# Attention over the heads: four slabs of head sums added by an accumulating DMA, and denominators taken three units behind

## The reference, cut to what matters

```python
def _L0_attn_b_ref(x, Wq, bq, Wk, bk, Wv, bv, Wo, bo):
    B, S, E = x.shape
    H = N_HEADS                      # 16 heads of D = 8
    D = E // H
    q = (x @ Wq.T + bq).reshape(B, S, H, D)
    k = (x @ Wk.T + bk).reshape(B, S, H, D)
    v = (x @ Wv.T + bv).reshape(B, S, H, D)
    scores = jnp.einsum('bqnd,bknd->bnqk', q, k) / jnp.sqrt(jnp.float32(D))
    attn = jax.nn.softmax(scores, axis=1)
    out = jnp.einsum('bnqk,bknd->bnqd', attn, v)
    out = out.transpose(0, 2, 1, 3).reshape(B, S, E)
    return out @ Wo.T + bo
```

## Time and profile before

| | us |
|---|---|
| median of 3 runs | 2010.51 |
| the profiled execution, its own time | 2014.26 |
| its span in the trace | 2012.4 |
| first and last L840 of the stage start at | 553.3 and 1691.9 |

### The profile page before, as it was taken

One profiled execution on the slowest core, in us unless ns is written; L12 is line 12 of the kernel. 1 busy time (PEld: TensorE's weight loads), 2 busy tenths in 40 slices (PEclk: granted clock), 3 DMA queues, 4 the chain that ended last, 5 costly groups with the idle time before them and its releaser, 6 DMA issues. The chain is left out here.

```text
span 2012.4 us, 54448 instructions
## 1 busy us (share of the span) xinstructions
PE 1915.1 (95%) x21688; PEld 1273.7 (63%) x21688; DVE 1715.0 (85%) x2601; ACT 1241.3 (62%) x2217; POOL 1547.4 (77%) x1180
## 2 busy tenths in 40 slices
PE   5998899999699999999999999999999998999998
PEld 3666644444367777777777777777777776544443
DVE  6776688886689999999999999999999997788876
ACT  4566456666466666666666666666666665566665
POOL 5255365656199999999999999999999997556565
PEclk8999799999799999999999999999999999799999
DMA  6744278564400000000000000000000000587762
GB/s 162 196 101 96 48 140 152 132 127 86 140 13 14 10 17 10 14 14 11 17 10 14 14 12 16 10 14 14 8 8 6 10 6 2 100 156 152 126 139 52
DMA packets 119886, 118.97 MB, mean 59 GB/s; under 512 B 50641, under 2 KB 82273, under 8 KB 118897
## 3 DMA queue, kind: packets, MB, share of 16 engines
q1 hardware_dynamic: 114112, 112.89, 25.9%
q10 hardware_dynamic: 5520, 2.60, 0.5%
HBM read 96.95 MB, written 18.55 MB: 57 GB/s over the span
## 5 line engine op out<-in xcount | busy, mean ns | idle before, releaser
L1099 DVE TENSOR_REDUCE head_shift<-head_score 128x64 bf16<-128x1024 f32 x512 | 624.1, 1219 | 81.8 <-PE head_score L883 69.8
L1056 ACT ACTIVATE head_ex<-head_score 128x1024 f32<-128x1024 f32 x512 | 524.7, 1025 | 185.3 <-PE head_score L905 183.5
L840 POOL TENSOR_TENSOR head_half<-head_ex 128x1024 f32<-128x1024 f32 x256 | 604.8, 2363 | 40.6 <-ACT head_ex L1056 40.6
L1355 POOL TENSOR_TENSOR ffn_sw<-ffn_sg,ffn_wide 128x512 f32<-128x512 f32 x256 | 325.0, 1269 | 218.7 <-ACT ffn_sg L1466 203.3
L1106 DVE TENSOR_TENSOR head_ex<-head_ex,head_recp 128x1536 f32<-128x1536 f32 x256 | 446.7, 1745 | 5.2 <-ACT head_recp L1028 5.2
L915 PE MATMUL head_den<-head_half,c_ident 128*128 128x128 f32 x3072 | 387.3, 276 | 2.5 <-POOL head_half L841 2.5
L915 PEld LDWEIGHTS head_den<-head_half,c_ident 128*128 128x128 f32 x3072 | 365.1, 193 | 6.0 <-POOL head_half L841 2.6
L847 POOL TENSOR_TENSOR head_ex<-head_ex,head_recip 128x512 f32<-128x512 f32 x256 | 329.0, 1285 | 22.6 <-ACT head_recip L1030 14.6
L905 PE MATMUL head_score<-head_shift,c_identb 128*128 128x512 bf16 x1024 | 310.0, 384 | 18.0 <-DVE head_shift L1099 12.0
L883 PE MATMUL head_score<-att_b_HB,att_b_GR 96*128 96x256 f16 x2048 | 311.5, 274 | 0.5 <-ACT head_ex L1056 0.5
L898 PE MATMUL head_outp<-head_ex,att_b_vs 128*32 128x128 f32 x8192 | 277.1, 276 | 0.0
(11 more groups left out here) (264 smaller groups left out, 2468.3 us busy)
## 6 DMA issues: line engine op xcount, KB each, us to landing
ffn_wide<-pair_weights SPq DMA_DIRECT2D x256, 256.0 KB, 9.7
band_v_windows<-a_values SPq DMA_DIRECT2D x24, 192.0 KB, 4.6
att_b_vs<-in_zero_f SPq DMA_DIRECT2D x2, 2176.0 KB, 10.2
a_keys<-band_parts_k SPq DMA_DIRECT2D x12, 295.5 KB, 2.5
att_a_HB<-a_keys SPq DMA_DIRECT2D x48, 73.9 KB
a_queries<-band_parts_q SPq DMA_DIRECT2D x12, 271.5 KB, 3.0
att_a_GR<-a_queries SPq DMA_DIRECT2D x12, 271.5 KB
b_queries<-head_parts_q SPq DMA_DIRECT2D x32, 96.0 KB, 1.6
```

Source lines behind the costliest of these rows:

```text
L840: ch.link(pool.tensor_tensor(hf, e[:, 0:8, :], e[:, 8:16, :], ALU.add))
L1056: act.activation(ex[:, kt % RING, :, h * QS:(h + 1) * QS], score[:, h, :, :].rearrange("p k (a w) -> p (k a) w", a=NH // 2), ACT.Exp, scal ...
L1099: dve.tensor_reduce(shift[:, h, :], score[:, h, :, :].rearrange("p k (a w) -> p w k a", a=NH // 2), AX.XY, ALU.max, negate=True).then_inc( ...
L1355: pool.tensor_tensor(sw[:, unit % 2, :], sg[:, unit % 2, :], wide[:, k % 2, i, :], ALU.mult).then_inc(sw_ready, 1)
```

## The change

The second sum on POOL (L841) goes. In its place POOL issues a DMA that adds slabs 4 to 7 of `half` onto its slabs 0 to 3, in SBUF, 512 f32 elements in each of 128 partitions (256 KB); the DMA engines do the addition. POOL issues it once its own first sum has been written (`half_ready`) and once the DMA of the unit before has landed (`quarters_added`). PE then waits for the DMA's semaphore and sums four slabs in place of six. LAG becomes 3, the ring of `ex` 5 buffers, and `half` 3 buffers (SUMS). The heads are stored in another order, so that the 12 slabs that DVE weighs and the 4 that POOL weighs each lie together; the numbers of elements stay as they were. PE's `attend` waits for POOL's four slabs before its 13th head, not before its 9th.

```diff
-    LAG, RING = 2, 4
-    ON_DVE = 3
-    SLABS = (0, 1, 4, 5, 6, 7)
+    LAG, RING, SUMS = 3, 5, 3
+    ON_DVE = 12
+    SLABS = range(NH // 4)
...
-            def sum_heads(unit, kt):
-
-                e, hf = ex[:, kt % RING, :, :], half[:, kt % 2, :, :]
-                ch = Chain(pool, pool_chain, unit)
+            def sum_heads(unit):
+
+                e, hf = ex[:, unit % RING, :, :], half[:, unit % SUMS, :, :]
                 pool.wait_ge(ex_ready, ONE + 2 * unit + 2)
-                pool.wait_ge(den_ready, ONE + unit)
-                ch.link(pool.tensor_tensor(hf, e[:, 0:8, :], e[:, 8:16, :], ALU.add))
-                pool.tensor_tensor(hf[:, 0:2, :], hf[:, 0:2, :], hf[:, 2:4, :], ALU.add).then_inc(quarter_ready, 1)
+                if unit >= SUMS:
+                    pool.wait_ge(den_ready, ONE + 1 + unit - SUMS + 1)
+                pool.tensor_tensor(hf, e[:, 0:8, :], e[:, 8:16, :], ALU.add).then_inc(half_ready, 1)
+                pool.wait_ge(half_ready, ONE + unit + 1)
+                if unit > 0:
+                    pool.wait_ge(quarters_added, unit * 16)
+                pool.dma_start(hf[:, 0:4, :], hf[:, 4:8, :], accum_op=ALU.add).then_inc(quarters_added, 16)
...
-                e = ex[:, kt % RING, :, :].rearrange("p (g a) q -> p g a q", a=GH)[:, :, ON_DVE, :]
-                pool.tensor_tensor(e, e, recip[:, kt % 2, :][:, None, :].broadcast_to([P, NG, P]),
+                e = ex[:, unit % RING, ON_DVE:NH, :]
+                pool.tensor_tensor(e, e, recip[:, unit % 2, :][:, None, :].broadcast_to([P, NH - ON_DVE, P]),
                                    ALU.mult).then_inc(rest_ready, 1)
...
-                    if i == HH:
+                    if i == ON_DVE:
                         pe.wait_ge(rest_ready, ONE + unit + 2)
...
-                pe.wait_ge(quarter_ready, ONE + unit + 1)
+                pe.wait_ge(quarters_added, (unit + 1) * 16)
                 pe.wait_ge(ln_done, ONE + unit)
                 for i, k in enumerate(SLABS):
-                    last = pe.matmul(den[:, 0:P], c["ident"][:, :], half[:, kt % 2, k, :], start=(i == 0), stop=(i == len(SLABS) - 1))
+                    last = pe.matmul(den[:, 0:P], c["ident"][:, :], half[:, unit % SUMS, k, :], start=(i == 0), stop=(i == len(SLABS) - 1))
```

More of the change, by code:

```diff
@@ L739, in head_softmax_attention @@
         ex = m.sb("ex", [P, RING, NH, P])
-        half = m.sb("half", [P, 2, NH // 2, P])
+        half = m.sb("half", [P, SUMS, NH // 2, P])
         recip = m.sb("recip", [P, 2, P])
@@ L832, in _, with weigh_rest @@
             m.start(pool, "pool")
[L834 to L837 removed]
+            def sum_heads(unit):
+                e, hf = ex[:, unit % RING, :, :], half[:, unit % SUMS, :, :]
                 pool.wait_ge(ex_ready, ONE + 2 * unit + 2)
[L839 to L843 removed]
+                if unit >= SUMS:
[5 more added lines that the diff above has]
+                pool.dma_start(hf[:, 0:4, :], hf[:, 4:8, :], accum_op=ALU.add).then_inc(quarters_added, 16)
+            def weigh_rest(unit):
                 pool.wait_ge(copy_ready, ONE + unit + 1)
[L846 to L847 removed]
+                e = ex[:, unit % RING, ON_DVE:NH, :]
+                pool.tensor_tensor(e, e, recip[:, unit % 2, :][:, None, :].broadcast_to([P, NH - ON_DVE, P]),
                                    ALU.mult).then_inc(rest_ready, 1)
@@ L853, in chunk_of @@
                     if not (first and kt < LAG):
-                        weigh_rest(unit - LAG, (kt - LAG) % BT)
-                    sum_heads(unit, kt)
+                        weigh_rest(unit - LAG)
+                    sum_heads(unit)
             chunk_of(0, True)
@@ L860, in _ @@
             for kt in range(BT - LAG, BT):
-                weigh_rest(LAST * BT + kt, kt)
+                weigh_rest(LAST * BT + kt)
         @block.tensor
@@ L897, in attend @@
                     at = n * VSLOT + VSLOT - D - n4 * D
-                    last = pe.matmul(outp[g * 32:(g + 1) * 32, 0:P], vs[:, buf * BT + kt, at:at + 32], ex[:, kt % RING, n, :],
+                    last = pe.matmul(outp[g * 32:(g + 1) * 32, 0:P], vs[:, buf * BT + kt, at:at + 32], ex[:, unit % RING, i, :],
                                      start=(kt == 0 and n4 == 0), stop=(kt == BT - 1 and n4 == GH - 1), skip_group_check=True)
@@ L908, in take_maximum, with denominator_of @@
                 last.then_inc(shifted, 1)
-            def denominator_of(unit, kt):
-                pe.wait_ge(quarter_ready, ONE + unit + 1)
+            def denominator_of(unit):
+                pe.wait_ge(quarters_added, (unit + 1) * 16)
                 pe.wait_ge(ln_done, ONE + unit)
                 for i, k in enumerate(SLABS):
-                    last = pe.matmul(den[:, 0:P], c["ident"][:, :], half[:, kt % 2, k, :], start=(i == 0), stop=(i == len(SLABS) - 1))
+                    last = pe.matmul(den[:, 0:P], c["ident"][:, :], half[:, unit % SUMS, k, :], start=(i == 0), stop=(i == len(SLABS) - 1))
                 last.then_inc(den_ready, 1)
@@ L952, in chunk_of @@
                     if not (first and kt < LAG):
-                        denominator_of(unit - LAG, (kt - LAG) % BT)
+                        denominator_of(unit - LAG)
                     if kt < BT - 1:
@@ L1019, in high_part, with reciprocal_of @@
                 return act.activation(parts, bank[:, None, :].broadcast_to([P, 2, cols]), ACT.Identity, bias=c["b_bias"][:, u:u + 1])
-            def reciprocal_of(unit, kt):
+            def reciprocal_of(unit):
                 act.wait_ge(copy_ready, ONE + unit)
@@ L1029, in reciprocal_of @@
                 act.wait_ge(rest_ready, ONE + unit)
-                act.activation(recip[:, kt % 2, :], lnd[:, :], ACT.Exp, scale=-1.0).then_inc(copy_ready, 1)
+                act.activation(recip[:, unit % 2, :], lnd[:, :], ACT.Exp, scale=-1.0).then_inc(copy_ready, 1)
             def copy_out(n):
@@ L1055, in chunk_of @@
                             act.wait_ge(av_done, ONE + unit)
-                        act.activation(ex[:, kt % RING, :, h * QS:(h + 1) * QS],
-                                       score[:, h, :, :].rearrange("p k (a w) -> p (k a) w", a=NH // 2),
+                        act.activation(ex[:, unit % RING, :, h * QS:(h + 1) * QS].rearrange("p (a g) w -> p g a w", g=NG),
+                                       score[:, h, :, :].rearrange("p k (g a w) -> p (k g) a w", a=GH, w=QS),
                                        ACT.Exp, scale=SCALE / ASCALE ** 2).then_inc(ex_ready, 1)
@@ L1061, in chunk_of @@
                         if h == 0 and not (first and kt < LAG):
-                            reciprocal_of(unit - LAG, (kt - LAG) % BT)
+                            reciprocal_of(unit - LAG)
                     ahead(b, q, kt)
@@ L1076, in _ @@
             for kt in range(BT - LAG, BT):
-                reciprocal_of(LAST * BT + kt, kt)
+                reciprocal_of(LAST * BT + kt)
             copy_out(LAST)
@@ L1100, in largest, with weigh @@
                                   AX.XY, ALU.max, negate=True).then_inc(shift_ready, 1)
-            def weigh(unit, kt):
+            def weigh(unit):
                 dve.wait_ge(recip_ready, ONE + unit + 2)
-                e = ex[:, kt % RING, :, :].rearrange("p (g a) q -> p g a q", a=GH)[:, :, 0:ON_DVE, :]
-                dve.tensor_tensor(e, e, recp[:, 0:P][:, None, None, :].broadcast_to([P, NG, ON_DVE, P]), ALU.mult).then_inc(prob_ready, 1)
+                e = ex[:, unit % RING, 0:ON_DVE, :]
+                dve.tensor_tensor(e, e, recp[:, 0:P][:, None, :].broadcast_to([P, ON_DVE, P]), ALU.mult).then_inc(prob_ready, 1)
             def add_output(n):
@@ L1150, in chunk_of @@
                     if not (first and kt < LAG):
-                        weigh(unit - LAG, (kt - LAG) % BT)
+                        weigh(unit - LAG)
                     ahead(b, q, kt)
@@ L1203, in _ @@
             for kt in range(BT - LAG, BT):
-                weigh(LAST * BT + kt, kt)
+                weigh(LAST * BT + kt)
             stats_of(LAST - 1)
```

6 lines of the change are left out of this document (3 added, 3 removed).

## The result

The changed kernel takes 2122.48 us (median of 4 runs, 2120.81 to 2123.71) against 2011.03 us before (median of 4 as well): a ratio of 1.055 (95% interval 1.054 to 1.057). The forecast was 2070 us, its own range 2025 to 2160 and the 8-in-10 range 1957 to 2230. The sign and the engine that sets the pace came out as forecast. The loss did not: 111 us, where the sum had 58.

A forecast was written before the change was run, and what follows sets the result against it. POOL alone was to bound the stage, at 4.68 us a unit against 4.465: 55 us over 255 distances plus 3 for edges, 2014.26 + 58 = 2072, less 3.75, say 2070 us; own range 2025 to 2160, 8-in-10 range 1957 to 2230.

The forecast's parts named there:

- PE's two matmuls: PE's denominator in each unit: four of six matmuls remain, 0.50 us less, so PE needs 3.91 us, not 4.41.
- PE's wait for the landing: PE's wait for the DMA before the denominator: some two units (9 us) remain for the landing, easier than POOL's wait.
- DVE's floor of 4.15 to 4.23: DVE's need per unit, 4.23 us with full projections and 4.15 in the last batch, the floor whatever POOL does.
- rival 1: Issue on POOL cheap or made beside its next instruction, DVE bounds: 1957 to 1960 us; chance 0.29 with its weaker form.
- I, the issue on POOL: Time one DMA issue holds POOL: 1.00 us taken, ends 0.34 and 3.5, making POOL's unit 3.68 + 1.00 = 4.68 us.
- the DMA needs the same wait: On POOL, the 0.08 us after L840 in which its write is awaited was taken to hold for the DMA too.
- the entries counted for the issue: POOL's issue: two reads and a write for each of 128 partitions, 384 entries at 2.13 ns, 0.18 + 0.82 us.
- The wait for the DMA before: POOL's wait before each issue: landing taken as 4.2 us against 4.68 between issues, 0.5 us of cover, so no cost.
- Edges: End of the stage: the last DMA costs 3.5 us more, two matmuls less give back 0.5; sum 3 us.
- 2: Rival: the landing takes over 4.68 us and sets the unit's length; at 5.3 us, 2228 us; chance 0.17.
- 3: Rival: the two prices on POOL cancel, issue between about 0.76 and 0.80 us; 2007 to 2014 us; chance 0.07.
- The signs: L840's distance near 4.68 us in all batches, gap to L847 1.0 us or more, DVE and PE about 90% and 83% busy.

The follow-up runs named there:

- no_dma: The changed kernel without the DMA and its wait, PE still summing four slabs, so half of the heads are missing from the denominator: 1970.49 us, ratio 0.9788.
- plain copy: The changed kernel with the same DMA without accumulation, so four slabs of sums are lost from the denominator: 2036.34 us in a single run.
- half_rows: The changed kernel with its DMA over 64 of the 128 partitions, the other half of the additions left out: 2100.63 us in a single run.
- two_flight: The changed kernel with each DMA waiting for that of two units before, not one, by two alternating semaphores: 2107.33 us, ratio to before 1.0474.
- dma_later: The changed kernel with POOL issuing each unit's DMA after its next product, the same instructions otherwise: 2039.42 us, ratio 1.0134.

## Why the prediction was right, and where its size was off

- **What bounds the stage.** Right: POOL alone after the change, PE and DVE with room. No_dma shows the cover: without the issue the same program ran at 4.30 us a unit.
- **PE's two matmuls.** Right in size, worth nothing: in the earlier trace rows the denominator was 1.50 us a unit, now 285.5 / 256 = 1.12 in the page, and PE waits 97.4 us for POOL. The 1.12 is spread by waits inside; an undisturbed one takes 1.06 us.
- **PE's wait for the landing.** The two units of cover weren't there: PE stood 42.2 us in 46 places for the DMA, in the rows above for the one that POOL had issued last. As POOL sets the pace, the other engines run ahead of it until they wait. It cost nothing, since POOL's product waited only 3.6 us for ACT.
- **DVE's floor of 4.15 to 4.23.** Never reached; 4.30 in no_dma. The allowance of 8 us for rival 1 was too small by about 10: it said 1957 to 1960, and no_dma took 1970.
- **I, the issue on POOL: the mis-sized term.** Put at 1.00 us; the undisturbed unit is 4.80 - 3.68 = 1.12. From the issue to the next start it is only 0.61 us. But from the start of L840 to the issue it is 2.95 us where it was 2.44 to L841: 0.29 for the late part of the issue before, which L840's end carries, and 0.22 for the longer wait (0.30 against 0.08). 0.61 + 0.29 + 0.22 = 1.12. The plain copy has the first and the last alone: 4.50 - 3.68 = 0.82, and 0.61 + 0.22 = 0.83. The step "the DMA needs the same wait" failed, and the entries counted for the issue weren't what it costs (half_rows), so 1.00 lay near by luck. 0.12 x 255 = 31 us of the miss.
- **The wait for the DMA before.** Put at nothing, with 0.5 us of cover below a landing of 4.2. It left out the 0.53 us at least that lie between a landing and the next issue's start: 4.2 + 0.53 = 4.73 would have been above its own 4.68. The median landing of 3.3 us saved it, which was luck. The tail reached 6.0 us, beside the 16 KB packets of the instruction queue. (4.882 - 4.80) x 255 = 21 us is what it and the waits without a name cost: beyond the usual 0.30 us, 20.5 - 20 x 0.30 = 14.5 in the 20 waits for a landing, which two_flight got back, and 7.6 - 6 x 0.30 = 5.8 in the six others, which it kept. One landing was compared with the room, where the longest should have been, with the time from landing to issue added.
- **Edges.** 2122.52 - 2014.26 = 108.3 us between the profiled executions, less (4.882 - 4.465) x 255 = 106.3, leaves 2; the sum had 3.
- **Added up.** 55 forecast + 31 + 21 = 107 of pace, against 106.3 measured.
- **Rivals.** 2 happened in part (15 us), 1 and 3 did not.
- **The signs.** The distance of L840 is 4.89, 4.89, 4.87 and 4.88 us in the four batches, so the last is as slow as the first, as said, and 0.2 above the 4.68. From the end of L840 to the next product it is 0.90 us, not 1.0 and more, because L840's record is itself 0.29 longer. DVE and PE are busy 87% and 88%, not 90% and 83%.
- **The rules of the Trainium skill.** "DMA: Bandwidth & Descriptors" (Specifications) gives about 1 us to the first byte of a GpSimd DMA. The reading by which that whole microsecond holds POOL is near the 1.12 us measured; the other, by which only 0.4 us would be added (a unit of 4.42), is not. The same page's 2.0 us plus the bytes (Anatomy of one DMA) gave 2.6 to 3.2 us for the landing, near the 3.3 measured, and 0.3 above the 2.3 of the plain copy; it says nothing of the tail that made the stalls.

## What to carry to other kernels

When work is taken off an engine by a DMA that the same engine issues, weigh the issue against the instruction removed: here 1.1 us replaced 0.68. The issue's price hardly changed between 64 and 128 rows, so let one issue do as much as its landing allows and shrink the engine's own work by as much. Issue it where the engine needn't wait for its own last result (0.6 us in place of 1.1), and let more than one be in flight; then compare the longest landing, not the median, with the room.

## What the runs showed that I had not expected

- An accumulating DMA holds POOL for 0.88 us by its record, a plain one for 0.58 us, and half the rows save only 34 ns.
- The next POOL instruction starts 0.61 us after an accumulating issue, before that record ends, and the records after it are about 0.3 us longer until a wait. Where the issue doesn't wait for its own sum (dma_later), the sum's record grew from 2.36 to as much as 3.3 us.
- Ordering alone was worth 83 us of 2122, although in that order the landing of the DMA before held four issues of five.
- Every DMA of POOL that took more than 4.02 us to land in the changed kernel had a 16 KB packet of the instruction queue beside it.
